# Moving the gate's base projection ahead of the small transposes in a recurrent-attention layer, with the next slot's front behind the output projection

## What is computed

```python
xn = _layernorm(x)
# recurrence
q, k, v = xn @ W_q.T, xn @ W_k.T, xn @ W_v.T         # q, k: 8 heads of 64
b = (q * k).sum(-1) * SCALE                          # per head
a = -softplus(xn @ W_alpha_w.T + W_alpha_b).sum(-1)  # per head
def step(carry, inp):
    ln, nm, sg = carry                               # state in logarithms
    ln = logaddexp(a_t + ln, b_t)
    ssum = sg * exp(a_t + nm - m) + sign(v_t) * exp(b_t + log|v_t| - m)
    ...                                              # y_t: heads summed
s = y @ W_o.T
# gate
result = xn @ base_w.T + base_b
gating = softmax(xn @ router_w.T + router_b).astype(bfloat16)
lora_out = einsum('bsr,erd,bse->bsd', xn @ lora_A, lora_B, gating)
g = silu(result + lora_out * 2)
out = x + s * g
```

## Time and profile before

| | us |
|---|---|
| median of the timed runs (2) | 1327.56 |
| lowest and highest | 1325.21, 1329.92 |
| the profiled execution, its own time | 1327.51 |
| its span, slowest core | 1326.0 |
| spans of the 8 cores | 1320.9 to 1326.0 |

### The profile page before, as it was taken

The page is one execution under the profiler, slowest core; times in us unless marked ns, Lnnn a source line. Parts: engine busy times, 40 slices in busy tenths (PEclk is TensorE's granted clock), DMA queues, the critical chain, the costliest instruction groups (busy, mean ns, idle before and its releaser), DMA issues.

```text
span 1326.0 us, 13629 instructions; the slowest of 8 cores (1320.9 to 1326.0 us)
## 1 busy us (share of the span) xinstructions
PE 906.3 (68%) x3936; PEld 379.0 (29%) x4000; DVE 519.3 (39%) x1191; ACT 449.6 (34%) x838; POOL 109.4 (8%) x124
## 2 busy tenths in 40 slices
PE   1100077787777877777787777877777778777885
PEld 0000033333333333333333333333333333333332
DVE  0000134444444443444444444444444444444443
ACT  2223123333333323333333333333323333333332
POOL 3000000000000000000000000000000000000000
PEclk9555578887788877878888888888878898788877
DMA  3444100000010000000000000000000000001000
GB/s 116 144 152 142 58 17 33 33 33 32 17 33 33 32 17 32 33 33 32 32 33 33 16 33 33 33 17 33 32 33 32 33 33 32 33 17 33 33 1 32
DMA packets 17806, 53.90 MB, mean 41 GB/s; under 512 B 3044, under 2 KB 3300, under 8 KB 17734
## 3 DMA queue, kind: packets, MB, share of 16 engines
q1 hardware_dynamic: 9792, 33.82, 7.2%
q10 hardware_dynamic: 7942, 19.21, 4.5%
HBM read 36.12 MB, written 16.91 MB: 40 GB/s over the span
## 4 chain that ended last, share of the span: by engine, by line
PE 30%; DVE 24%; issue 16%; ACT 15%; DMA 11%; DVEq 1%; ACTq 1%; POOLq 0%; POOL 0%; SPq 0%
PE pv L611 12%; DVE wstf L676 5%; ACT L757 3%; ACT bsc L757 2%; DVE ncsf L726 2%; PE pq L661 2%; ACT xnt_h L457 2%; PE pal L743 2%; PE pk L661 2%; ACT xnf L469 2%; PE pw L743 2%; DVE bsc L667 2%; DVE bsc L759 2%; DVE xnf L525 2%; DVE xnf L523 2%
## 5 line engine op out<-in xcount | busy, mean ns | idle before, releaser
L611 PE MATMUL pv<-wb_h,xnt_h 128*128 128x512 bf16 x512 | 171.9, 496 | 34.1 <-DVE g_h L603 34.1
L765 POOL TENSOR_TENSOR xb<-bsc,xb 128x1024 f32<-128x1024 f32 x32 | 76.3, 2385 | 753.7 <-DVE bsc L762 753.7
L743 PE MATMUL pal<-wo_h,yt_h 128*128 128x512 bf16 x224 | 104.2, 610 | 30.4 <-ACT yt_h L719 24.5
L418 PE MATMUL pv<-wv_h,xnt_h 128*128 128x512 bf16 x511 | 116.0, 380 | 0.1
L667 DVE TENSOR_TENSOR bsc<-pq,m0r 128x512 f32<-128x512 f32 x32 | 22.1, 692 | 212.2 <-PE pq L661 212.2
L611 PEld LDWEIGHTS pv<-wb_h,xnt_h 128*128 128x128 bf16 x512 | 59.9, 121 | 132.0 <-issue 106.9
L418 PE MATMUL t<-rm_h,xnt_h 128*128 128x16 bf16 x256 | 11.2, 170 | 118.2 <-DMA rb<-yt_h 118.2
L507 PE MATMUL pq<-wq_h,xnt_h 128*128 128x512 bf16 x256 | 67.2, 385 | 33.9 <-ACT wq_h L334 16.6
L713 PE MATMUL pal<-wst_h,vh_h 128*128 128x128 bf16 x128 | 18.7, 300 | 96.6 <-ACT wst_h L681 96.6
L537 ACT ACT_TABLE_LOAD x31 | 39.8, 1283 | 128.5 <-DVE nmx L534 128.5
L743 PE MATMUL pw<-wo_h,yt_h 128*128 128x512 bf16 x256 | 75.4, 421 | 4.8 <-PE pw L743 1.4
(11 more groups left out here) (142 smaller groups left out, 1385.2 us busy)
## 6 DMA issues: line engine op xcount, KB each, us to landing
xb<-x SPq DMA_DIRECT2D x32, 512.0 KB, 3.4
out<-xb SPq DMA_DIRECT2D x32, 512.0 KB, 2.7
bsc<-wv ACTq DMA_DIRECT2D x4, 512.0 KB, 3.4
xb<-wv ACTq DMA_DIRECT2D x4, 512.0 KB
bsc<-wb ACTq DMA_DIRECT2D x4, 512.0 KB, 3.5
xb<-wb ACTq DMA_DIRECT2D x4, 512.0 KB
bsc<-wo ACTq DMA_DIRECT2D x4, 512.0 KB, 3.3
xb<-wo ACTq DMA_DIRECT2D x4, 512.0 KB
```

Source lines behind the costliest of these rows:

```text
L418: last = e.matmul(dest_ap, xnth(k), wh[:, co:co + nblk], start=(k == 0), stop=(k == KCH - 1 and extra is None))
L611: e.matmul(dst, xnth(k), T["wb_h"][:, co:co + 512], start=(k == 0), stop=False)
L743: last = e.matmul(dst, T["yt_h"][:, k * 128:(k + 1) * 128], T["wo_h"][:, co:co + 512], start=(k == 0), stop=(k == KCH - 1))
L765: E("pool", lambda e, xt=xt: e.tensor_tensor(xt[:], T["bsc"][:], xt[:], op=ALU.add), reads=[T["bsc"], xt], writes=[xt])
```

## The change

Two things move; no operation is added or removed.

The gate projection's 8 base matmuls of each half are a group of their own (ubase), emitted straight after the two copies of v out of pv and before the transpose of av. The 2 matmuls with g65_h of each half stay at the old place (ulora), and no longer read xnt_h or wb_h.

front_ln and front_tr are one function again, called from the loop after mid and before back. In mid the state update follows the output projection instead of preceding it.

```diff
+            for hf in range(2):
+                def ubase(e, hf=hf):
+                    dst = T["pv"][:, hf * 512:(hf + 1) * 512]
+                    last = None
+                    for k in range(KCH):
+                        co = k * 1024 + hf * 512
+                        last = e.matmul(dst, xnth(k), T["wb_h"][:, co:co + 512],
+                                        start=(k == 0), stop=False)
+                    return last
+                E("pe", ubase,
+                  reads=[T["xnt_h"], T["wb_h"]],
+                  writes=[(T["pv"], f"h{hf}")])
             E("pe", lambda e: e.transpose(T["t1"][0:8, 0:128], T["av"][:], T["idf"][:]),
...
             for hf in range(2):
-                def umm(e, hf=hf):
+                def ulora(e, hf=hf):
                     dst = T["pv"][:, hf * 512:(hf + 1) * 512]
-                    for k in range(KCH):
-                        co = k * 1024 + hf * 512
-                        e.matmul(dst, xnth(k), T["wb_h"][:, co:co + 512],
-                                 start=(k == 0), stop=False)
                     sl = slice(hf * 512, (hf + 1) * 512)
                     e.matmul(dst, T["g65_h"][:], T["lb_h"][:, sl], start=False, stop=False)
                     return e.matmul(dst, T["g65_h"][:], T["lb_l"][:, sl], start=False, stop=True)
-                E("pe", umm,
-                  reads=[T["xnt_h"], T["wb_h"],
-                         T["g65_h"], T["lb_h"], T["lb_l"]],
+                E("pe", ulora,
+                  reads=[T["g65_h"], T["lb_h"], T["lb_l"]],
                   writes=[(T["pv"], f"h{hf}")])
...
-            for hf, bank in [(0, "t0"), (1, "t1")]:
-                E("dve", lambda e, hf=hf, bank=bank, ncf=ncf: e.scalar_tensor_tensor(
...
-            E("act", lambda e, nch_=nch_, ncf=ncf: e.activation(out=nch_[:], in_=ncf[:],
-                                                                func=AF.Copy),
-              reads=[(ncf, "h0"), (ncf, "h1")], writes=[nch_])
-
-            front_ln(si + 1)
-
             for hf, bank in [(0, SBANKS[0]), (1, SBANKS[1])]:
...
-            front_tr(si + 1)
+            for hf, bank in [(0, "t0"), (1, "t1")]:
+                E("dve", lambda e, hf=hf, bank=bank, ncf=ncf: e.scalar_tensor_tensor(
...
+            E("act", lambda e, nch_=nch_, ncf=ncf: e.activation(out=nch_[:], in_=ncf[:],
+                                                                func=AF.Copy),
+              reads=[(ncf, "h0"), (ncf, "h1")], writes=[nch_])
...
         load_slot(0)
-        front_ln(0)
-        front_tr(0)
+        front(0)
         emit_prep()
         for si in range(NS):
             mid(si)
+            front(si + 1)
             back(si)
```

More of the change, by code:

```diff
@@ L459, in tr_batch, with front @@
                   reads=[tp], writes=[(dh_res, f"h{half}")])
-        def front_ln(si):
+        def front(si):
             if si >= NS:
@@ L489, in front_ln @@
               reads=[xt, T["rstd"], T["mrstd"]], writes=[T["xnf"]])
-        def front_tr(si):
-            if si >= NS:
-                return
             tr_batch(T["xnf"], T["xnf"], T["xnt_h"], T["xnt_h"], 0)
@@ L723, in mid @@
               reads=[T["pw"]], writes=[(T["yt_h"], "h1")])
-            for hf, bank in [(0, "t0"), (1, "t1")]:
-                E("dve", lambda e, hf=hf, bank=bank, ncf=ncf: e.scalar_tensor_tensor(
-                    ncf[:, hf * 512:(hf + 1) * 512], ncf[:, hf * 512:(hf + 1) * 512],
-                    T["epend"][:], T[bank][0:8, 0:512], op0=ALU.mult, op1=ALU.add),
-                  reads=[(ncf, f"h{hf}"), T["epend"], T[bank]], writes=[(ncf, f"h{hf}")])
-            E("act", lambda e, nch_=nch_, ncf=ncf: e.activation(out=nch_[:], in_=ncf[:],
-                                                                func=AF.Copy),
-              reads=[(ncf, "h0"), (ncf, "h1")], writes=[nch_])
-            front_ln(si + 1)
             for hf, bank in [(0, SBANKS[0]), (1, SBANKS[1])]:
@@ L749, in mid @@
                       writes=[T[bank]])
-            front_tr(si + 1)
+            for hf, bank in [(0, "t0"), (1, "t1")]:
+                E("dve", lambda e, hf=hf, bank=bank, ncf=ncf: e.scalar_tensor_tensor(
+                    ncf[:, hf * 512:(hf + 1) * 512], ncf[:, hf * 512:(hf + 1) * 512],
+                    T["epend"][:], T[bank][0:8, 0:512], op0=ALU.mult, op1=ALU.add),
+                  reads=[(ncf, f"h{hf}"), T["epend"], T[bank]], writes=[(ncf, f"h{hf}")])
+            E("act", lambda e, nch_=nch_, ncf=ncf: e.activation(out=nch_[:], in_=ncf[:],
+                                                                func=AF.Copy),
+              reads=[(ncf, "h0"), (ncf, "h1")], writes=[nch_])
         def back(si):
```

## The result

The changed kernel takes 1439.05 us (median of 9 runs); the kernel before took 1327.92 beside it (8 runs). The ratio is 1.0843, 95% interval 1.0824 to 1.0863: slower by 8.4%. Some executions are slowed, the cores of one die running longer at a lower clock: the medians here count them, the ratios and their intervals leave them out. The profiled execution took 1437.72 us, its slowest core (7) has a span of 1436.1. The forecast was 1432, within 1395 to 1450.

A forecast was written before the change was run, and what follows sets the result against it. It took a long chain of dependent steps across all engines to bound the kernel. A later start (1.5 us) and half clock (1.74 us) at the decay matrices, 32 slots, added 104 us to 1327.5: 1432 us, range 1395 to 1450.

The forecast's parts named there:

- The front and the state update cost nothing: Moving both behind the output projection leaves every engine's order and waits the same: cost 0.
- (a): The 16 base matmuls start behind the copies of v, first at +11.6 us in the slot, last ending at +15.2.
- (b): The transpose of av and the ladder of tiny dependent steps behind it go 3.1 us late; selc issued at +21.96.
- Step (c): TensorE stands waiting for selc's DMA; the decay matrices start at +23.7 instead of +22.2, +1.5 us a slot.
- Step (d): The thin stretch ahead drops TensorE to 1.2 GHz, so the decay matrices take 1.74 us more a slot.
- step (e): Full clock in the gate projection's first half shortens only TensorE's own queue; output projection and next opening move together: gain 0.
- The higher bound of 2.1: Upper end for the decay matrices' half-clock cost, 2.1 us, from another float32 pair's 0.13 us per 128 columns.
- The sum: Late start plus half clock at the decay matrices: 1.5 + 1.74 = 3.25 us a slot, 32 slots, 104 us.
- Full clock at the decay matrices: Rival: the decay matrices stay at 2.4 GHz, only their late start costs: 48 us, 1376 us; chance 0.10.
- The rule of the Trainium skill: Rival: closing the hole behind the V projection saves 1.35 us a slot, 1284 us; faster by either way 0.03.

The follow-up runs named there:

- the version kept warm: The changed kernel with 18 more matmuls per slot, results unread, filling TensorE's idle time ahead of the decay matrices: 1395.25 us, ratio 1.0557.

## Why the prediction was right

**The front and the state update cost nothing.** Confirmed by itself: 1.0002.

**Steps (a) and (b), the start and the shift.** Right to 0.1 us: first base matmul at 730.03 - 718.37 = +11.66 (+11.6 forecast), the transpose of av at +15.12 (+15.1), the ladder 740.40 - 733.49 = 6.91 us (6.86).

**Step (c), the cover gone.** Right: selc's landing releases the decay matrices in 32 of 32 places, 1.72 us after the issue (1.7 forecast), at +23.75. The wait is 62.9 us in total, a shade under the 2 us in each slot that I had named. That this wait decides is shown by the version with two buffers and two semaphores, 2.0 us a slot less. The four matmuls with g65_h, at half clock, ran from 737.26 to 739.13 and took 1.87 us instead of the 0.9 forecast; the wait for selc covers it.

**Step (d), the clock.** Right in kind and size: all 128 matmuls at 1052 ns or more. From the decay matrices to the next opening the changed kernel takes 39.54 - 23.7 = 15.8 us on average, against the 14.0 of before: +1.8, forecast +1.74. In the slot with the clock kept it is 239.63 - 225.71 = 13.92 us, the same 13.92 as in the earlier trace rows, and the version with half of the matmuls ahead shows the longer time, 15.71, without the later start. The slot shown above takes more, 39.81 - 23.75 = 16.06:

```profile
756.88 0.81 DVE L487 TENSOR_SCALAR xnf<-xb,rstd,mrstd 128x1024 f32<-128x1024 f32 x1
...
758.18 1.04 PE L452 MATMUL t<-idf,xnf 128*128 128x128 f32 x8
```

The opening comes 1.30 us after the start of L487, where it comes 0.96 us after it at 718.37 (757.84 would be the same here): TensorE was still in the output projection. So in this slot step (e) is 0.34 us short; the kernel before has such slots too (14.24 us in the earlier trace rows). One row I misread: the 0.58 in the earlier trace rows is the mean over 3.3 us, and 0.58 means some five sixths of that time at 1.2 GHz, not half. The higher bound of 2.1 from the earlier trace rows was too high, as the text supposed.

**Step (e), no gain from the base matmuls' full clock.** Right for the changed kernel, but for the slots just named. But it hid the larger finding, below.

**The sum.** Forecast +3.25 us a slot, measured +3.36, which over 32 slots makes 3.5 us of the 5.7 by which 1437.7 passes 1432. The rest, some 2 us, lies in the start-up, on two different cores: the second slot opens 5.45 us later than before (203.87 against 198.42), of which the first slot's share is 3.4.

**The rivals.** Full clock at the decay matrices (1376): out, but the mean of the version kept warm, 1395, shows what that case looks like. The rule of the Trainium skill that idle gaps between matmul bursts should be kept shut ("TensorE: Matmul & The Clock Gate", section "Why this matters for your kernels"): it is borne out in its direction by the runs that shut them with bf16 matmuls, 1.0843 to 1.0557 in the changed kernel and 1.000 to 0.974 in the one before, and not by the one that put thin float32 matmuls into the wait, 1.001. What was wrong was only to read the change as one that shuts a gap; it moved the gap to a worse place.

**What the prediction didn't see.** I wrote that the selc transfer is hidden in the kernel before and its cover is the gate projection. True, but the kernel before holds 1.2 us a slot that the gate projection takes because its first half runs at half clock. The rows for it stood in the earlier trace rows, 3.24 beside 1.89 us; I used them only to say what the change does not gain.

Left open: why, in the version with the base matmuls in the waits, the clock at the decay matrices holds in some slots and falls in others. Their work and offsets overlap. What part of the wait for selc has to be filled isn't known either: the 8 matmuls that took half of it kept the clock in most slots, and the 4 left it as it was.

## What to carry to other kernels

Before moving a block of work into a wait, look at what is queued behind it on its engine: a wait inside a chain of small dependent steps can be filled between the steps, in pieces as long as each wait, but not ahead of the first, where all of the block's length is added to the chain. And find out what the moved block was covering; here it hid a DMA transfer and kept TensorE's clock up for the float32 matmuls that follow. Check in the list of waits that a filler shortens the wait it is meant for: a small step in the middle, as the transpose of eet here, can split a hole in two. Where the clock falls in a hole, filling the hole can be worth more than the work moved.

## What the runs showed of the hardware

Two fillers that kept TensorE busy for the same time left it with different clocks. Two thin float32 matmuls as filler (8 rows) didn't hold it for the decay matrices, periods of 35.42 to 36.23 on the eight cores; bf16 matmuls on all 128 rows for the same time did in most slots, 34.76 to 35.08. Whether the rows in use or the data type makes the difference wasn't tried apart.

Once lost, the clock takes time to come back, even under steady work. In the changed kernel the decay matrices (float32, 9 of 128 rows in use) kept TensorE busy for 3.78 of 3.80 us at 0.50 throughout; in the kernel before, bf16 matmuls ran at 0.50 for 4.95 us. Whether decay matrices that ran on for longer would win it back isn't shown.

Float32 matmuls follow the clock like others: a pk pair starts its second 0.43 us after the first at 2.4 GHz (1.02 less 0.587) and 0.85 us at 1.2 GHz (1.91 less 1.056).

Work that nobody reads made a kernel faster: 11 matmuls of 512 columns per slot, 352 in all, took 34 us off (1290.61 against 1325.04).
